# Moving the state's low half from GpSimd to the vector engine in a four-layer graph network, with the stages' orders as explicit lists

## What is computed

```python
x = layernorm(x + gnn0(x, adj))        # exp(8*tanh(x q k' x' / s)) * adj, row-normalised, times x v
x = layernorm(x + gnn1(x, adj))        # sigmoid edges, self part, two linear maps
x = layernorm(x + gnn2(x, adj))        # relu(sum_k T_k(adj) x W_k)
def step(h):                           # layer 3, five times
    m = adj @ h                        # in and out matrices are both adj: av = [m, m]
    z = sigmoid(av @ w3.T + h @ u3.T)
    r = sigmoid(av @ w4.T + h @ u3.T)
    hv = tanh(av @ w5.T + (r * h) @ u5.T)
    return (1 - z) * h + z * hv
x = layernorm(x + step^5(x))
```

## Time and profile before

| | us |
|---|---|
| median of 3 runs (2039.12 to 2041.62) | 2041.39 |
| the profiled execution, whole | 2039.13 |
| its span, first to last instruction | 2036.8 |
| mean granted TensorE clock | 0.962 of full |
| busy: TensorE / vector / ScalarE / GpSimd | 1856.7 / 1472.1 / 1354.7 / 921.1 |

### The profile page before, as it was taken

One profiled execution on the slowest core, in us unless ns is written; L12 is line 12 of the kernel. 1 busy time (PEld: TensorE's weight loads), 2 busy tenths in 40 slices (PEclk: granted clock), 3 DMA queues, 4 the chain that ended last, 5 costly groups with the idle time before them and its releaser, 6 DMA issues.

```text
span 2036.8 us, 27531 instructions
## 1 busy us (share of the span) xinstructions
PE 1856.7 (91%) x9307; PEld 1442.9 (71%) x9307; DVE 1472.1 (72%) x3054; ACT 1354.7 (67%) x2689; POOL 921.1 (45%) x1009
## 2 busy tenths in 40 slices
PE   3899998899998999889998899989999889989997
PEld 2776776777767777577775777757768677676775
DVE  6786688766687667866778667786667866678666
ACT  0766677576766767566775667756768666686666
POOL 2354445445364442634436344363444544345344
PEclk6999999999999999999999999999999999999998
DMA  2000001000010000100000000100001000000000
GB/s 69 22 1 0 1 1 42 1 1 1 7 37 1 1 1 12 32 1 0 1 24 21 1 1 1 43 1 1 1 2 42 0 1 1 2 22 1 0 1 22
DMA packets 13514, 21.32 MB, mean 10 GB/s; under 512 B 2720, under 2 KB 5024, under 8 KB 13216
## 3 DMA queue, kind: packets, MB, share of 16 engines
q1 hardware_dynamic: 10768, 18.68, 2.7%
q10 hardware_dynamic: 2576, 0.53, 0.1%
HBM read 10.82 MB, written 8.39 MB: 9 GB/s over the span
## 4 chain that ended last, share of the span: by engine, by line
PE 65%; DVE 13%; issue 8%; POOL 7%; ACT 7%; DMA 0%; DVEq 0%; SPq 0%; POOLq 0%; ACTq 0%
PE psA L1080 7%; PE psA L1050 7%; PE psA L1051 7%; PE psA L881 5%; PE psB L886 5%; PE psB L888 5%; PE psB L887 5%; PE psA L886 3%; PE psA L888 3%; PE psA L887 3%; PE psB L949 3%; PE psA L949 3%; DVE E L753 2%; ACT X L471 2%; PE psB L1074 2%
## 5 line engine op out<-in xcount | busy, mean ns | idle before, releaser
L430 POOL TENSOR_TENSOR S<-S,H 128x512 f32<-128x512 f32 x160 | 225.1, 1407 | 486.3 <-ACT S L573 486.3
L1050 PE MATMUL psA<-adjT_hi,nh_hi 128*128 128x512 f32 x640 | 275.0, 430 | 11.9 <-ACT H L559 11.6
L471 ACT ACTIVATE X<-X,shift,rstd 128x128 f32<-128x128 f32 x512 | 210.4, 501 | 90.2 <-POOL shift L401 89.2
L1051 PE MATMUL psA<-adjT_hi,nh_lo 128*128 128x512 f32 x640 | 259.8, 406 | 0.0
L425 POOL TENSOR_TENSOR xT_lo<-H,xT_hi 128x512 fp32r<-128x512 f32 x160 | 219.2, 1383 | 71.0 <-ACT xT_hi L581 38.1
L841 DVE SCALAR_TENSOR_TENSOR E<-E 128x512 f32<-128x512 f32 x160 | 181.7, 1135 | 63.3 <-ACT E L577 60.4
L836 DVE SCALAR_TENSOR_TENSOR E<-E,H 128x512 f32<-128x512 f32 x160 | 128.5, 803 | 115.1 <-ACT E L567 114.7
L679 DVE TENSOR_TENSOR gT_lo<-psA,gT_hi 128x512 fp32r<-128x512 f32 x160 | 108.8, 688 | 115.0 <-ACT gT_hi L563 101.1
L396 POOL TENSOR_TENSOR neg_mean<-zero_cols,mv 128x4 f32<-128x4 f32 x128 | 30.8, 240 | 356.1 <-DVE mv L696 355.8
L1080 PE MATMUL psA<-E,u5T 128*128 128x512 f32 x320 | 165.0, 597 | 13.7 <-DVE E L836 13.7
L571 ACT ACTIVATE E<-psB,z_bias 128x512 f32<-128x512 f32 x160 | 110.4, 690 | 81.3 <-PE psB L1074 79.8
(11 more groups left out here) (224 smaller groups left out, 5317.1 us busy)
## 6 DMA issues: line engine op xcount, KB each, us to landing
xin<-in_x SPq DMA_DIRECT2D x32, 256.0 KB, 3.0
out<-X SPq DMA_DIRECT2D x32, 256.0 KB, 2.0
E<-in_adj SPq DMA_DIRECT2D x1, 1024.0 KB, 5.7
E<-in_L_gnn_w_w SPq DMA_DIRECT2D x3, 128.0 KB, 7.2
E<-in_L_gnn_weight SPq DMA_DIRECT2D x1, 192.0 KB, 6.8
E<-in_L_gnn_u_w SPq DMA_DIRECT2D x2, 64.0 KB, 6.9
Wm_sb<-in_L_gnn_Wm ACTq DMA_DIRECT2D x1, 128.0 KB, 7.0
E<-in_L_gnn_q SPq DMA_DIRECT2D x1, 64.0 KB, 5.5
```

What stands on the lines that cost most here:

```text
L430: nc.gpsimd.tensor_tensor(kept[s], kept[s], H[s][:, :], ALU.mult).then_inc(pool_done[s], 1)
L471: last = nc.scalar.activation(X[s][:, t, :], X[s][:, t, :], ACT.Identity, scale=rstd[s][:, t:t + 1], bias=shift[s][:, t:t + 1])
L1050: nc.tensor.matmul(psA[s][:, :], hi, adjT_hi[:, m, :], start=(m == 0), stop=False)
L1051: last = nc.tensor.matmul(psA[s][:, :], lo, adjT_hi[:, m, :], start=False, stop=(exact and m == TILES - 1))
```

## The change

Two things. First, the subtraction `xT_lo` = H - `xT_hi` of the five recurrent steps goes from GpSimd's stage m to the vector engine, as a new part of stage uh with the same waits; TensorE's uh now waits for the vector engine's semaphore. Second, `SCHEDULE`, `LAGS` and the formula are replaced by `ORDER`, a list of stage.slot for each engine, where a leading "-" stands for behind. On TensorE and ScalarE the lists hold the same parts as the formula gave, in another order in places; on the vector engine there are 20 parts more (uh), on GpSimd 20 fewer (m). Cut to where the orders differ most and to what the prediction speaks of:

```diff
-SCHEDULE = [
-    ("x0", 9.81, 8.54, 8.09, 41.84),
...
-]
+ORDER = {
+    "tensor": (
...
+        "uh4.0 r4.0 t3.2 v4.0 m4.1 rh4.0 t3.3 uh4.1 r4.1 m4.2 v4.1 uh4.2 r4.2 t4.0 rh4.1 m4.3 v4.2 t4.1 rh4.2 uh4.3 "
+        "r4.3 "
+    ),
+    "scalar": (
+        "-m4.3 -v4.2 -rh4.2 x0.0 -r4.3 -v4.3 x0.1 -rh4.3 x0.2 query.0 query.1 scores01.0 query.2 x0.3 scores01.1 "
...
+        "t3.3 split3.3 rh4.0 r4.1 m4.2 v4.1 r4.2 rh4.1 "
+    ),
+    "vector": (
+        "-r4.2 -m4.3 -last.1 -spread3.0 -rh4.2 -r4.3 x0.0 -last.2 -spread3.1 -rh4.3 x0.1 -spread3.2 query.0 x0.2 "
...
+        "sums0.0 spread0.0 scores23.2 scores01.3 scores23.3 sums0.1 spread0.1 sums0.2 x1.0 spread0.2 sums0.3 x1.1 "
+        "spread0.3 xh.0 xh.1 gates.0 x1.2 x1.3 edges.0 xh.2 gates.1 edges.1 gates.2 xh.3 sums1.0 edges.2 gates.3 "
...
+        "cheb23.2 cheb23.3 lap1.1 lap_lo.1 lap1.3 lap_lo.3 lap2.1 spread2.0 spread2.1 lap2.3 x3.0 spread2.3 spread2.2 "
+        "uh0.0 x3.1 uh0.1 m0.0 x3.2 uh0.2 x3.3 r0.0 m0.1 m0.2 uh0.3 m0.3 r0.1 r0.2 rh0.0 r0.3 rh0.1 t0.0 rh0.2 t0.1 "
...
+        "m4.0 t3.1 rh3.3 t3.2 r4.0 uh4.2 uh4.1 m4.1 t3.3 uh4.3 r4.1 rh4.0 m4.2 last.0 rh4.1 "
+    ),
...
 def body(engine):
...
+    out = []
+    for token in ORDER.get(engine, "").split():
+        name, slot = token.lstrip("-").split(".")
+        out.append((name, int(slot), int(token.startswith("-"))))
+    return out
...
-            def stage_m(s, r, k):
-
-                pool.wait_ge(xT_hi_ready[s], XT_HIS * r + XT_HI["x3" if k == 0 else f"h{k - 1}"])
-                if k == 0:
-                    pool.wait_ge(copied[s], COPIES * r + COPIED["x3"])
-                nc.gpsimd.tensor_tensor(xT_lo[s][:, :], H[s][:, :], xT_hi[s][:, :].bitcast(F32), ALU.subtract).then_inc(pool_done[s], 1)
-
...
+            def stage_uh(s, r, k):
+                dve.wait_ge(xT_hi_ready[s], XT_HIS * r + XT_HI["x3" if k == 0 else f"h{k - 1}"])
+                if k == 0:
+                    dve.wait_ge(copied[s], COPIES * r + COPIED["x3"])
+                lo_part(xT_lo[s][:, :], H[s][:, :], xT_hi[s][:, :]).then_inc(vector_done[s], 1)
+
...
-                pe.wait_ge(pool_done[s], POOLS * r + POOL[f"h_lo{k}"])
+                pe.wait_ge(vector_done[s], VECTORS * r + VECTOR[f"h_lo{k}"])
```

More of the change, by code:

```diff
@@ L108 @@
[L108 to L114, removed]
-    return SCHEDULE[n][LAGS[engine]] if engine in LAGS else 0.0
-def body(engine):
-    period = sum(length for _, length in STAGES) + SLOT_LAG
-    at = []
-    for s in range(SLOTS):
-        time = (s // 2) * PAIR_LAG + (s % 2) * SLOT_LAG
-        for n, (name, length) in enumerate(STAGES):
-            if name == "lap1" and s % 2 == 0 or name == "spread2" and s % 2 == 1:
-                time += SLOT_LAG
-            if name not in ("lap1", "lap_lo", "lap2") or s % 2:
-                t = time + elag(engine, n)
-                at.append((t % period, s, n, name, int(t // period)))
-            time += length
-    assert all(behind in (0, 1) for *_, behind in at)
-    return [(name, s, behind) for _, s, _, name, behind in sorted(at)]
+ORDER = {
+    "tensor": (
[12 rows of a table added]
+    ),
+    "scalar": (
[12 rows of a table added]
+    ),
+    "vector": (
[12 rows of a table added]
+    ),
+    "gpsimd": (
[4 rows of a table added]
+    ),
+}
@@ L156 @@
     ["rsum", "elu_low1", "elu1", "src_bias", "self", "elu_low2", "elu2"]
-    + [f"{name}{k}" for k in range(STEPS) for name in ("rh", "update", "h")])}
+    + [f"{name}{k}" for k in range(STEPS) for name in ("h_lo", "rh", "update", "h")])}
 POOL = {name: n + 1 for n, name in enumerate(
@@ L160 @@
      "neg_mean1", "var1", "rstd1", "shift1", "bias2", "neg_mean2", "var2", "rstd2", "shift2"]
-    + [f"{name}{k}" for k in range(STEPS) for name in ("h_lo", "kept")] + ["neg_mean3", "var3", "rstd3", "shift3"])}
+    + [f"{name}{k}" for k in range(STEPS) for name in ("kept",)] + ["neg_mean3", "var3", "rstd3", "shift3"])}
 TURNS, XTS, GTS, NHS, COPIES, PRODUCTS, VECTORS, POOLS = map(len, (TURNED, XT, GT, NH, COPIED, PRODUCT, VECTOR, POOL))
@@ L436, in _ @@
             for k in range(STEPS):
-                stages[f"m{k}"] = lambda s, r, k=k: stage_m(s, r, k)
                 stages[f"v{k}"] = lambda s, r, k=k: stage_v(s, r, k)
@@ L866, in _ @@
                 stages[f"m{k}"] = lambda s, r, k=k: stage_m(s, r, k)
+                stages[f"uh{k}"] = lambda s, r, k=k: stage_uh(s, r, k)
                 stages[f"r{k}"] = lambda s, r, k=k: stage_r(s, r, k)
```

## The result

The changed kernel is slower: 2059.29 us median (2050.54 to 2061.56, 5 runs) against 2040.31 (2039.12 to 2041.62, 5 runs) of the kernel before, a ratio of 1.0084 with a 95% interval of 1.0062 to 1.0106. Forecast were 2023 us with a range to 2047. The profiled execution lasted 2059.29 us.

A forecast was written before the change was run, and what follows sets the result against it. TensorE, 91% busy, was taken as the bound, with 26 us a round lost to gaps and low clock. Terms 1.2 + 0.6 + 0 + 0.5 = 2.3 us a round, x 8 = 18 us, gave 2023 us, range 2003 to 2047.

The forecast's parts named there:

- the round's end: Last stretch of a round: slot 2's gated state comes earlier and TensorE's wait shortens, 1.2 us a round gained, bounds 0 and 2.1.
- layer 1: TensorE's 1.64 us wait for slot 0's low half goes, slot 3's norm is late next: 0.6 us a round gained.
- the middle: Layer 2, norm and step 0: layer 2's products 0, step 0 ends 0.5 us a round earlier, bounds 0 and 0.8.
- The moved operation: Low-half subtraction on the vector engine: 0.69 us each, 110 us added, 52 us back from update lines less held by GpSimd.
- its own 1.06 may be 0.69: Round's end: slot 2's gated state itself runs shorter on the vector engine, 0.37 us of the 2.1 us on this chain.
- the two before it: Round's end: state update falls from 1.80 to 0.69 us (1.11 earlier); gated state stands first behind the loop's turn (0.61 earlier).
- Layer 2's products: Slot 1's transpose ahead of slot 0's delays slot 0 by some 0.4 us, hidden: 0 us, bounds -0.4 and 0.2.
- The steps: Recurrent steps: TensorE is busy 100 of 100 us at full clock, stays full, and no reordering gives time back.
- held queue: Rival, recurrent steps: low halves, held by GpSimd's product, delay vector operations behind them, 35 us in all: 2058 us, chance 0.17.
- the clock comes back: Rival, layer 1 and round's end: shorter gaps end low-clock stretches, 3.2 us a round, 26 us more: 1997 us, chance 0.14.

The follow-up runs named there:

- e6: Kernel before with only the subtraction moved, old orders kept, all 20 low halves well placed: 2031.90 us, ratio 0.9963 to the kernel before.
- e11: e7 with the two vector stages behind the loop's turn swapped, slot 2's gated state ahead of slot 3's low half: 2027.90 us, 0.9953 to the kernel before.
- e9: Changed kernel with the round's end, next first products and softmax scores in the old order, low halves well placed: 2056.96 us, 1.0085 to the kernel before.
- e7: e6 with one more stage moved: slot 0's layer-1 low half ahead of slot 2's statistics on the vector engine: 2023.64 us, 0.9924 to the kernel before.
- e5: Changed kernel with layer 2's products back in the old order on all four engines: 2042.68 us, ratio 1.0017 to the kernel before.
- e12: e7 with layer 2's products alone in the new order on all engines: 2027.97 us, ratio 0.9949 to the kernel before.
- e15: Changed kernel with recurrent steps 0 to 3 in the old order, low halves well placed: 2046.25 us, ratio 1.0034 to the kernel before.
- e14: e7 with the round's end, first products and softmax scores in the new order on all engines: 2036.17 us, ratio 0.9990 to the kernel before.
- e1: Kernel before with the subtraction moved and old orders, in a first placement of the 20 low halves: 2054.72 us, ratio 1.0078 to the kernel before.
- e3: Changed kernel with layer 1 back in the old order on all four engines: 2050.50 us, ratio 1.0057 to the kernel before.

## Why the prediction was wrong

Forecast was a gain of 2.3 us a round, measured a loss of 2.5. The 4.8 us between them are three terms: the round's end (1.9), layer 1 (1.7) and the middle (1.3).

- **The moved operation**: right in kind. 690 ns each, as taken; the excess of the update lines fell by 45 us with the move alone, against 52. The vector engine's busy time came to 1522 us in e6 (1530 forecast) and to 1464 in the changed kernel, since the new orders bring fewer of its operations against GpSimd. That was of no use: the engine wasn't the bound.
- **Round's end, 1.2 us gain (0 to 2.1)**: failed; 0.7 us loss, outside the bounds. The step "its own 1.06 may be 0.69" and the two before it took the start of the gated state for what sets its end. It is GpSimd's product that sets it, at 1.81 us behind its start, in whatever order (e11, e9). With the gain at zero, the 0.7 us of cover that I saw go behind the wait is a plain loss: 2.19 + 0.70 = 2.89, as measured.
- **Layer 1, 0.6 us gain (-0.5 to 1.6)**: the mechanism was right for the one stage that I priced (e7: 0.64), and the sum failed since it held that stage alone. The change of TensorE's order behind it (gates ahead of aggregations) was named in no term, and neither was a fall of the clock that costs more than before. Measured 1.1 us loss; in the rounds in which the clock didn't fall late in the layer 0.2 gain, inside the bounds. The step that failed is the price of the low clock behind it, which I took as unchanged: 2 us in each round in which the fall came late.
- **Layer 2's products, 0 (-0.4 to 0.2)**: mis-sized: e5 and e12 give 0.3 to 0.4 loss, at the bound. The 0.30 us wait in step 0 did go, but the middle as a whole lost 0.8 where 0.5 gain was forecast; what made the part that isn't layer 2's order stays open.
- **The steps, nothing**: no idle time, as forecast, but 0.6 us a round against e6 (1.52 and 0.88) and 0.5 against e15, in small losses that no waits list shows. Against before they broke even (1.52 and 1.49), because the move's own gain there, 0.6, was used up.
- **The first products of the next round**: had no term at all. In e14 they cost 1.1 a round.
- **The rival "held queue"**: did not happen in the changed kernel, whose places are good. It is real: e1 has two of the 20 places wrong and is 23 us slower than e6, where the rival had 35. I had priced it by the tightest place; it struck where a queue met another engine's old order.
- **The rival "the clock comes back"**: half of it came. At the round's end and start it did come back (0.82 to 0.91 in the stretch at the end of the round shown, four later rounds that began at the fallen clock in place of six). In layer 1 the stretch kept its 0.97, and there I had the sign wrong: I took fallen clock as something that shorter gaps can only end, at a fixed price, while the same fall cost at most 0.3 us at its old place and 2 us at its new one.

What stays open: the one-by-one costs on top of e7 add up to 0.0081 + 0.0025 + 0.0048 + 0.0066 = 0.022, 45 us, while the changed kernel is 33 us behind e7, and undone one by one in the changed kernel (e15, e5, e3, e9) they return 0.0050 + 0.0067 + 0.0027 - 0.0001 = 0.0143, 29 us. The clock's falls are no sum of parts, and I can't say from these runs how much of each cost is order and how much is the instant at which the next stretch meets the clock. The table bounds it only where a stretch has no edit.

## What to carry over

Split a change that moves an operation and rewrites the orders: here the first was worth 8 to 11 us and the second cost 25 to 28, a part of it through the clock, and keeping the old orders with one stage moved (e7) is 0.76% faster than the kernel before and 1.6% faster than the changed one. Price a queue position by what stands behind it and by when the other engine's order delivers its input, and find out what sets the end of a held operation before you move its start. Where TensorE has gaps, compare kernels by stretch, and look in how many rounds the clock fell, and where in the stretch, before you credit an edit with a difference.
